# The last MLP of a graph kernel in fp32r throughout, and A's identity added by GpSimd

## The reference

```
ax1 = A @ x ; ax2 = A @ x2
h1 = (2 + eps1) * ax1 ; h2 = (2 + eps2) * ax2
for i in 0..2:  h1 = relu(h1 @ W1[i].T + b1[i]) ; h2 = relu(h2 @ W2[i].T + b2[i])
x = layernorm(x + concat(h1, h2) @ Wm.T + bm)
d = rsqrt(rowsum(A) + 1)
x = layernorm(x + (d * ((A + I) @ (d * x))) @ W.T + b)
```

## Time and profile before

| | |
|---|---|
| median of 3 runs | 591.12 us (590.76 to 591.52) |
| the profiled execution's own time | 591.38 us |
| its span, first to last instruction | 589.6 us |
| mean granted TensorE clock | 0.998 |
| TensorE busy (matmul) | 583.0 us, 99% |
| VectorE busy | 545.4 us, 93% |
| ScalarE busy | 378.8 us, 64% |
| GpSimd busy | 28.1 us, 5% |
| DMA | 141.91 MB, mean 241 GB/s |

### The profile page before, as it was taken

One profiled execution on the slowest core, in us unless ns is written; L12 is line 12 of the kernel. 1 busy time (PEld: TensorE's weight loads), 2 busy tenths in 40 slices (PEclk: granted clock), 3 DMA queues, 4 the chain that ended last, 5 costly groups with the idle time before them and its releaser, 6 DMA issues.

```text
span 589.6 us, 7659 instructions
## 1 busy us (share of the span) xinstructions
PE 583.0 (99%) x2676; PEld 485.9 (82%) x2676; DVE 545.4 (93%) x695; ACT 378.8 (64%) x512; POOL 28.1 (5%) x26
## 2 busy tenths in 40 slices
PE   9999999999999999999999999999999999999996
PEld 8888888888888888888888888878888888888885
DVE  6999999998988998898799999997999997989986
ACT  6544437852454773453667336479799799799794
POOL 0000000001100000110000020000200001010011
PEclk9999999999999999999999999999999999999999
DMA  8968565443655544354544374776899999999921
GB/s 330 397 248 294 206 223 206 145 148 143 207 196 179 179 169 145 142 197 178 195 147 143 143 268 187 261 287 222 316 365 392 425 377 340 387 338 367 387 77 72
DMA packets 31131, 141.91 MB, mean 241 GB/s; under 512 B 5504, under 2 KB 6272, under 8 KB 17024
## 3 DMA queue, kind: packets, MB, share of 16 engines
q1 hardware_dynamic: 30528, 139.87, 64.6%
q10 hardware_dynamic: 576, 1.70, 0.7%
HBM read 139.40 MB, written 2.16 MB: 240 GB/s over the span
## 4 chain that ended last, share of the span: by engine, by line
PE 97%; ACT 1%; DVE 1%; issue 1%; POOLq 0%; POOL 0%; DVEq 0%
PE ps L536 81%; PE pd L557 6%; PE ps L612 6%; PE pd L566 2%; PE pd L598 1%; PE pd L664 1%; ACT outn L756 0%; ACT ahi L723 0%; DVE z L1217 0%; ACT ahi_extra L723 0%; DVE stats L1222 0%; POOLq L124 0%; POOL rstd L1246 0%; DVE mv L1007 0%; DVE vareps L1014 0%
## 5 line engine op out<-in xcount | busy, mean ns | idle before, releaser
L723 ACT ACTIVATE ahi<-raw 128x1024 fp32r<-128x1024 f32 x212 | 222.6, 1060 | 162.5 <-PE ps L536 156.3
L920 DVE TENSOR_TENSOR alo<-raw,ahi 128x1024 fp32r<-128x1024 f32 x212 | 256.5, 1218 | 27.0 <-ACT ahi L723 26.0
L536 PE MATMUL ps<-ahi,x2s 128*128 128x512 f32 x512 | 138.4, 389 | 0.0
L536 PE MATMUL ps<-ahi,x1hi 128*128 128x512 f32 x384 | 121.9, 393 | 0.0
L536 PE MATMUL ps<-ahi,x1lo 128*128 128x512 f32 x384 | 120.9, 390 | 0.0
L536 PE MATMUL ps<-alo,x1hi 128*128 128x512 f32 x384 | 120.6, 390 | 0.0
L536 PEld LDWEIGHTS ps<-ahi,x2s 128*128 128x128 f32 x512 | 96.4, 188 | 20.1
L536 PEld LDWEIGHTS ps<-alo,x1hi 128*128 128x128 f32 x384 | 72.2, 188 | 15.1
L536 PEld LDWEIGHTS ps<-ahi,x1lo 128*128 128x128 f32 x384 | 72.3, 188 | 15.0
L536 PEld LDWEIGHTS ps<-ahi,x1hi 128*128 128x128 f32 x384 | 71.9, 188 | 15.0 <-issue 0.7
L536 PE MATMUL ps<-alo,x2s 128*128 128x512 f32 x256 | 80.2, 389 | 0.0
(11 more groups left out here) (103 smaller groups left out, 526.6 us busy)
## 6 DMA issues: line engine op xcount, KB each, us to landing
raw<-a_t SPq DMA_DIRECT2D x108, 1024.0 KB, 4.9
raw<-a_t SPq DMA_DIRECT2D x32, 512.0 KB, 7.4
raw<-early SPq DMA_DIRECT2D x7, 512.0 KB, 7.5
xn<-x SPq DMA_DIRECT2D x2, 1024.0 KB, 7.8
xn<-x SPq DMA_DIRECT2D x3, 512.0 KB, 10.5
out<-outn ACTq DMA_DIRECT2D x3, 512.0 KB, 6.6
par<-params SPq DMA_DIRECT2D x1, 708.0 KB, 12.4
raw<-head SPq DMA_DIRECT2D x2, 256.0 KB, 3.1
```

The lines of the kernel that those rows point to most:

```text
L536: mm = pe.matmul(ps[bank + (CH * (q % 2) if layer else 0)][:, :], block_of(w, n), a[c], start=(n == 0 and k == 0), stop=(n == JB - 1 and k ...
L723: act.activation(ring_hi(layer, q, n), raw_tile(layer, n), ACT.Copy).then_inc(hi_ready, 1)
L920: dve.tensor_tensor(ring_lo(layer, q, n), raw_tile(layer, n), as_f32(ring_hi(layer, q, n)), ALU.subtract).then_inc(lo_ready, 1)
```

## The change

The first layer of the last MLP is done with three fp32r products like all others. So ScalarE rounds the evacuated h in two parts (after its tiles 3 and 4), and VectorE splits it in two parts; the splits of the two other layers are also given in two parts. The steps are moved: TensorE's dense layers stand after steps 4, 6 and 8 and the merge after step 10; with the merge move the residual, the statistics (both by the formula in the tables), ScalarE's scaled y (step 20 to 24), its rounding and splitting (by 4) and the last normalisation (step 29 to 32). `add_identity` and `add_identities_last` move from VectorE to GpSimd, where they stand between the powers, each behind its wait for the data.

```diff
-PE_DENSE = ({3: 0, 5: 1, 8: 2}, {1: 0, 3: 1, 5: 2})
-PE_MERGE = (10, 6)
-DVE_SPLIT_H = {4: 1, 6: 2}
+PE_DENSE = ({3: 0, 5: 1, 8: 2}, {4: 0, 6: 1, 8: 2})
+PE_MERGE = (10, 10)
+DVE_SPLIT_H = {3: (0, 0), 4: (0, 2), 5: (1, 0), 6: (1, 2), 8: (2, 0), 9: (2, 2)}
...
-ACT_RELU = ({k + SPLIT: l for k, l in PE_DENSE[0].items()}, {4: 0, 6: 1, 7: 2})
+ACT_RELU = ({k + SPLIT: l for k, l in PE_DENSE[0].items()}, {7: 0, 9: 1, 10: 2})
...
-ACT_NORM_LAST = 29
+ACT_NORM_LAST = 32
...
-ACT_NORM = (22, 20)
+ACT_NORM = (22, 24)
-DVE_MAKE_Y = (KB + 4, 2 * KB + 4, 3 * KB + 3, 23)
+DVE_MAKE_Y = (KB + 4, 2 * KB + 4, 3 * KB + 3, 27)
...
                         passes = ((whi, hhi), (whi, hlo), (wlo, hhi))
-                    elif l:
-                        wait(pe, hlo_ready, q * (LAYERS * M) + (M * (l - 1) + m + 1))
+                    else:
+                        wait(pe, hlo_ready, q * (LAYERS * M) + (M * l + m + 1))
                         passes = ((whi, hhi), (whi, h_rest), (wlo, hhi))
-                    else:
-                        wait(pe, h_ready, q * (4 * M) + (M * l + m + 1))
-                        passes = ((par, h),)
...
-                if plan == 0 and n in (ACT_EVACUATE[0] + 1, ACT_EVACUATE[0] + 2):
+                if n in (ACT_EVACUATE[plan] + 1, ACT_EVACUATE[plan] + 2):
                     for m in range(CH):
-                        round_h(q, 0, CH * (n - ACT_EVACUATE[0] - 1) + m)
+                        round_h(q, 0, CH * (n - ACT_EVACUATE[plan] - 1) + m)
...
-                wait(dve, hhi_ready, q * (LAYERS * M) + (M * (l - plan) + m + 1))
+                wait(dve, hhi_ready, q * (LAYERS * M) + (M * l + m + 1))
...
                         if p in DVE_SPLIT_H:
-                            for m in range(M):
-                                split_h(LAST, DVE_SPLIT_H[p], m, 1)
+                            l, first = DVE_SPLIT_H[p]
+                            for m in range(first, first + CH):
+                                split_h(LAST, l, m, 1)
...
-                    if JB <= p and (p - JB + AHEAD2) // KB == 1:
-                        add_identity(1, p - JB + AHEAD2)
...
+            for n in range(KB):
+                add_identity(0, n)
             degree_power(QUARTERS - 1)
             norm_power(QUARTERS)
-            for q in range(QUARTERS - 1):
-                norm_power(q + QUARTERS + 1)
+            for n in range(KB, 2 * KB):
+                add_identity(1, n)
+            for q in range(2, QUARTERS):
+                if q == LAST:
+                    for n in range(JB):
+                        if squares_of(n):
+                            add_identities_last(n)
+                    norm_power(2 * QUARTERS - 1)
+                else:
+                    norm_power(QUARTERS + 1)
+                    for n in range(q * KB, q * KB + KB):
+                        add_identity(q, n)
+                    norm_power(QUARTERS + q)
```

More of the change, by code:

```diff
@@ L97 @@
 DVE_SECOND_BASE = DVE_SPLIT_Y[:2] + (JB + 26, 2 * JB + 28)
-AHEAD = 3
-AHEAD2 = 5
 DVE_RESIDUAL2 = PE_PROJECT + SPLIT2
@@ L1088, in y_step @@
                         second_base(g)
[L1090 to L1102, removed]
             def residual2(q, k):
@@ L1147, in layer0_quarter @@
                         y_step(n, range(QUARTERS - 1))
-                        if n >= JB - KB:
-                            add_identity(0, n + KB - JB)
             def layer1_first():
@@ L1174, in layer1_quarter @@
                         second_base(3)
[L1175 to L1180, removed]
             dve.memset(blank[:, :], 0.0).then_inc(blank_ready, 1)
@@ L1241, in degree_power, with add_identity, add_identities_last @@
                 pool.tensor_tensor(degpow[:, :], degc[:, :], halves[:, :], ALU.pow).then_inc(degpow_ready, 1)
+            def add_identity(q, n):
+                wait_raw1(pool, q, n)
+                k = n % KB
+                square = raw_tile(1, n)[:, k * P:(k + 1) * P]
+                pool.tensor_tensor(square, square, identity[:, :], ALU.add).then_inc(identity_added, 1)
+            def add_identities_last(n):
+                wait_unit(pool, n)
+                for at in squares_of(n):
+                    square = raw_tile(1, n)[:, at:at + P]
+                    pool.tensor_tensor(square, square, identity[:, :], ALU.add).then_inc(identity_added, 1)
             def norm_power(done, r=slice(0, KB)):
```

## The result

The changed kernel takes 592.79 us (median of 9 runs, 592.08 to 593.58), the kernel before 591.33 us (9 runs, 590.58 to 592.13): 1.0023 times as long, 95% interval 1.0014 to 1.0032. That is clear of no change, but not clear of 0.2%, the least that the prediction calls slower. The profiled execution took 592.54 us, its span is 590.7 us, the mean granted clock 0.999. The forecast was 592.9 us, slower. The sum came out near; several of its terms did not, as the stages show. Of the 27 executions of the kernel before that stand beside the first four experiments two were slow (1202.72 and 1257.59 us); the ratios leave them out, and the median of all, 591.64, would be 591.62 without them.

What follows compares the result with a forecast made beforehand. TensorE's own pace was taken as the bound until the tail. Terms -0.71 + 0.31 + (1.77 + 0.36) + 0.23 - 0.23 = +1.7 us gave 593.1 profiled, 592.9 as median; range 590.4 to 594.6.

Steps and rivals of the forecast that it cites:

- dense layer in fp32r: Last MLP's first dense layer on TensorE: twelve fp32r products (2.72 us) replace eight fp32 records (3.43), gaining 0.71 us.
- 1.77 + e: TensorE's stall for VectorE at layer 1's tiles 3 and 4: 1.77 us plus e, the shift of VectorE's position.
- last y, adds of quarter 1: Where VectorE splits the last y, two of GpSimd's adds meet 0.3 us of margin: 0.23 us of stall.
- The first new wait: Layer 1, tiles 3 and 4 now come at once; VectorE's row sum and splits stop TensorE for 1.77 + e.
- e = 8 x 0.25 - 1.64 = +0.36: VectorE's shift before layer 1: eight GpSimd adds each hold it 0.25 us, against 1.64 us of its own adds removed.
- The second new wait: Loop of dense layer 0, activation, split and tile 6: VectorE's tile comes late for TensorE, stall 0.31 us.
- The 0.23 us of the tail are won.: In the tail VectorE's chain comes out earlier against TensorE, so TensorE's 0.23 us wait for VectorE disappears.
- the six other adds: Quarter 1's remaining GpSimd adds: 1.5 us of VectorE delay, set against 0.23 us gained per tile over nine tiles.
- fall where VectorE waits for ScalarE: GpSimd's adds of quarter 2 were placed in VectorE's waits for ScalarE; no term in the sum.
- GpSimd hides: Rival: GpSimd's adds cost VectorE nearly nothing (hold per add h = 0); not slower, 590.6 us; chance 0.42.
- The whole lock: Rival: each GpSimd add holds VectorE for its whole operation, 0.48 us; +4.9 us, 596.0 us; chance 0.12.
- The last y: Rival: the last y comes late and tile 32 waits; needs 3 us further delay; given no chance of its own.

Runs made afterwards that it cites:

- the first four experiments: Changed kernel with only its MLP part (594.14 us), only its adds (591.37), quarter 1's adds back on VectorE (593.03), or VectorE's last row sum later (592.05).
- MLP alone: The kernel before with only the MLP half of the change, all identity adds left on VectorE: 594.14 us, ratio 1.0042.
- The two halves: The kernel before with only the MLP tables and layers changed (594.14 us), and with only the identity adds moved to GpSimd (591.37 us).
- the table's eight kernels: The changed kernel (592.79 us) and seven follow-up kernels whose stage shifts against the kernel before were tabulated; kernels with bursts stopping TensorE in layer 0 left out.

## Why the prediction was right, and where it was not

The sum by its terms. All measured values are from the profiled execution, less its own offset.

| term | predicted | measured |
|---|---|---|
| dense layer in fp32r | -0.71 | -0.69 |
| stops at tiles 3 and 4 (1.77 + e) | +2.13 | +1.10, and 0.22 for two restarts |
| stop at tile 6 | +0.31 | +0.31, and 0.11 for the restart |
| last y, adds of quarter 1 | +0.23 | +0.50 |
| merge | 0 | -0.05 |
| tail | -0.23 | 0 |
| sum | +1.73 | +1.50; the last matmul stands at +1.46, the rest is rounding of the starts |

- **The dense layer.** Right. Before, 8.87 us of TensorE's time went into the dense layers and the slow first product behind the fp32 ones (3.43 + 2 x 2.72); the three fp32r layers now take 2.73 + 2.73 + 2.72 = 8.18.
- **The first new wait.** The mechanism and the place were right, and 1.77 + e holds within 0.12 us in the MLP alone (1.65) and in the changed kernel (1.10 against 1.22 for its e). The step that failed is "e = 8 x 0.25 - 1.64 = +0.36". The hold was right (0.27 for 0.25), the eight were not: four got in, the fifth starved until VectorE had done with its full stretch and the last three queued behind it, and e was -0.55. (The third and fourth tiles' data came at 357.34 and not before 354, which changed nothing.)
- **The second new wait.** 0.31 us, as worked out, and it stayed when VectorE's position was moved. What the sum had put at nothing is the restart, 0.11 us for each of the three stops.
- **The adds of quarter 1.** Right that two of them reach TensorE; but VectorE's pace of 1.40 against TensorE's 1.36 goes on over all eight, so 0.50 for 0.23 us.
- **"The 0.23 us of the tail are won."** Wrong. The prediction set the six other adds against 0.23 us a tile of catching up over nine tiles, and let VectorE be early in the tail. It had moved the merge by four tiles without taking these four off VectorE's catching up (0.92 us), and so took the tail for TensorE's. The two halves show it: MLP alone the end is late by 2.42 us where TensorE is late by 1.55 at tile 42. In the changed kernel the adds taken off VectorE in quarters 2 and 3 pay most of that back: its split is late by 2.41 us at tile 70, by 1.52 at tile 80 and by 1.47 at the last one. The prediction gave the adds of quarter 2 nothing ("fall where VectorE waits for ScalarE"), but in the kernel before they stand at 504.63 to 514.96 us in a stretch of VectorE without a pause:

```profile
504.63 0.29 DVE L1095 TENSOR_TENSOR raw<-raw,identity 128x128 f32<-128x128 f32 x1
504.84 1.22 DVE L920 TENSOR_TENSOR alo_extra<-raw,ahi_extra 128x1024 fp32r<-128x1024 f32 x1
```

- **The rivals.** "GpSimd hides" with h = 0 falls as a price: no add that got in was free in the full stretches. The four adds of quarter 0 that didn't get in cost VectorE nothing, though, which is why e came out between the forecast's and this rival's. The whole lock falls too: 0.27 us of hold for an add that takes 0.46. The last y wasn't late.

So 592.9 against 592.79 us is partly luck: the first stops came 1.03 us smaller, and the restarts, the y stage and the tail 0.83 us larger (0.33 + 0.27 + 0.23). As a difference the forecast was +1.73 and the measured one +1.46; the times lie nearer to each other because the kernel before measured 591.33 beside the changed one and not 591.12. With e = -0.55 and nothing else changed, the forecast would have been 0.91 lower, about 592.0, inside the range, and within 0.2% of the time before.

## What to carry to other kernels

When a step is moved later on a nearly full engine, take away from that engine's catching up what the move costs (tiles moved times the difference of the two paces), and look whether that engine's pauses are waits for something that itself waits for it, for in these nothing is caught up. Ask at the end of the kernel which engine's last piece the end hangs on: here it was VectorE's last split in seven of the table's eight kernels, though TensorE was busy for 99% of the span. An operation handed from VectorE to GpSimd isn't free while VectorE reads two inputs: a small add saved 0.205 us of VectorE's pitch and put a hold of 0.27 in its place, so here the move paid only where an add met a pause, a short operation or one with a single SBUF input, as most of quarters 2 and 3 did (by the stages of the changed kernel).

## What the runs showed of the hardware

- One add of 128x128 in fp32 on GpSimd takes 0.46 us when it is free to run. Let in between VectorE's two-input operations, it holds the next one by 0.27 us (two tiles, in place) or 0.20 (one tile twice, another written), not by its length. The Trainium skill (SBUF — State Buffer, Who interferes with whom) says that who comes first has the shared pair for the whole instruction and the other blocks fully. In one direction the trace agrees: a queued add runs only once VectorE's current operation is over, so a burst of them takes VectorE's pitch (16 adds in 21.73 us, 1.36 each). In the other it doesn't, and the measurement decides: VectorE's hold is 0.20 to 0.27 of the 0.46 us.
- An add of GpSimd that came out of idling at 376 us found no place for 14 to 15 us among VectorE's operations, in each of the seven kernels that had GpSimd idle there (14.84 us in the changed one, 14.45 to 14.88 in six others), whatever it read. Behind other adds it got in at once, and out of idling at other places too. Such a wait shows as busy time of GpSimd, never as idle, and a reader who takes the 1569 ns of the group for the add's price is wrong by a factor of three.
